# A graph network on one core: a matrix cleared with 28 stores instead of 14, and filled from three chunks later

## The reference

```python
h = relu(layernorm(x)); f = h @ W_n                        # 8 heads of 32
e = leaky(left[src] + right[dst] + edge terms) / 3         # a score per edge and head
a = exp(e - max over dst) / sum over dst                   # softmax over the edges of a node
x = x + segment_sum(f[src] * a, dst)                       # attention layer
h = relu(layernorm(x))
for l in range(3):                                         # three message layers
    msg = relu(h @ pW[l] + pb[l])[src]
    mean = segment_sum(msg, dst) / max(degree, 1)
    out = mean @ lW[l] + lb[l] + h @ rW[l]
    h = out / norm(out)                                    # silu behind the first two
return x + layernorm(h) * ln_w + ln_b
```

## Time and profile before

| | us |
|---|---|
| median of three runs | 3459.19 |
| lowest and highest of them | 3453.91, 3459.5 |
| profiled execution, its own time | 3451.81 |
| its span in the trace | 3450.0 |
| attention stage of GpSimd, first gather to last scattered write | 101.7 to 1457.4 |
| busy in the span: TensorE, GpSimd, VectorE, ScalarE | 2900.8, 2527.9, 1542.9, 1377.4 |

### The profile page before, as it was taken

One profiled execution on the slowest core, in us unless ns is written; L12 is line 12 of the kernel. 1 busy time (PEld: TensorE's weight loads), 2 busy tenths in 40 slices (PEclk: granted clock), 3 DMA queues, 4 the chain that ended last, 5 costly groups with the idle time before them and its releaser, 6 DMA issues. The chain is left out here.

```text
span 3450.0 us, 44783 instructions
## 1 busy us (share of the span) xinstructions
PE 2900.8 (84%) x12845; PEld 1770.6 (51%) x12845; DVE 1542.9 (45%) x5381; ACT 1377.4 (40%) x3235; POOL 2527.9 (73%) x2655
## 2 busy tenths in 40 slices
PE   7688877777777777199999997999999888999984
PEld 5577656656555655044455553444555433445542
DVE  6399655555555556113333232232333423445445
ACT  5366655555554555033333332333333322222220
POOL 2677777777777777777777776777777767777775
PEclk9688988888888888599999999999999999999995
DMA  7898766666666664166666654666666456667663
GB/s 218 228 281 256 204 171 178 171 169 174 179 168 177 173 169 125 42 195 182 184 194 194 201 173 143 183 180 183 199 196 201 147 171 190 197 199 221 208 187 108
DMA packets 491898, 631.26 MB, mean 183 GB/s; under 512 B 163477, under 2 KB 402096, under 8 KB 491648
## 3 DMA queue, kind: packets, MB, share of 16 engines
q0 software_dynamic: 122192, 324.68, 34.0%
q1 hardware_dynamic: 340848, 277.92, 27.2%
q10 hardware_dynamic: 28608, 25.71, 2.3%
HBM read 558.00 MB, written 70.05 MB: 182 GB/s over the span
## 5 line engine op out<-in xcount | busy, mean ns | idle before, releaser
L1218 POOL DMA_INDIRECT ring<-message_table,src_index x1545 | 1469.8, 951 | 502.5 <-issue 481.1
L1269 PE MATMUL ps<-ring,attention_work 128*128 128x384 f32 (+1 forms) x2940 | 1149.5, 538 | 85.3 <-DMA attention_work<-message_table 75.1
L604 POOL DMA_INDIRECT ring<-attention_table,src_index x784 | 763.1, 973 | 245.6 <-issue 245.2
L1269 PEld LDWEIGHTS ps<-ring,attention_work 128*128 128x128 f32 x2940 | 551.5, 192 | 555.7 <-issue 286.4
L1814 PE MATMUL ps<-ring,one_hot 128*128 128x265 f32 x1568 | 533.1, 458 | 19.7 <-issue 18.6
L1580 ACT ACTIVATE ring<-one_hot 128x384 f32<-128x384 uint8 (+1 forms) x735 | 362.0, 553 | 195.7 <-PE ps L1269 132.9
L1814 PEld LDWEIGHTS ps<-ring,one_hot 128*128 128x128 f32 x1568 | 314.7, 221 | 85.6 <-issue 49.6
L1339 PE MATMUL ps<-ring,attention_work 128*32 128x256 f32 x3090 | 256.6, 402 | 103.7 <-DMA ring<-message_table,src_index 103.4
L613 POOL DMA_INDIRECT dense_adjacency<-times,cell x277 | 269.5, 973 | 84.4 <-issue 84.4
L1434 DVE SCALAR_TENSOR_TENSOR block_o<-ps,inv_deg,root 128x256 f32<-128x256 f32 x147 | 71.1, 484 | 546.8 <-PE ps L1307 546.8
L1783 PE MATMUL ps<-ring,ident 128*128 128x224 f32 x224 | 95.7, 519 | 254.7 <-DMA ring<-attention_table,src_index 254.6
(11 more groups left out here) (185 smaller groups left out, 3500.7 us busy)
## 6 DMA issues: line engine op xcount, KB each, us to landing
attention_work<-message_table SPq DMA_DIRECT2D x360, 256.0 KB
attention_work<-in_dst_edges SPq DMA_DIRECT2D x112, 448.0 KB
ring<-message_table,src_index POOLq DMA_INDIRECT x1545
one_hot<-dense_adjacency SPq DMA_DIRECT2D x63, 336.0 KB, 4.0
one_hot<-dense_adjacency SPq DMA_DIRECT2D x42, 448.0 KB, 4.5
attention_sums<-sums_out SPq DMA_DIRECT2D x112, 132.5 KB
dense_adjacency<-root SPq DMA_DIRECT2D x14, 952.0 KB
ring<-attention_table,src_index POOLq DMA_INDIRECT x784
```

The costliest lines, as they stand in the source:

```text
L604: pool.indirect_dma_start(m.ring[:, k, t, 0:cols], None, table, bass.IndirectOffsetOnAxis(ap=m.src[:, at:at + 1], axis=0)).then_inc(s[f"ro ...
L1218: pool.indirect_dma_start(m.quad_ring[:, k, j, :], None, m.tables[w.l], bass.IndirectOffsetOnAxis(ap=m.src[:, t:t + 1], axis=0)).then_inc( ...
L1269: last = nc.tensor.matmul(m.ps[:, 2 + half, 0:cols], m.m_rows[:, u % HELD_ROWS, half * P:(half + 1) * P], m.a_rows[:, k, 0:cols], start=(j ...
```

## The change

The matrix is cleared with 28 stores of two pieces each, one in each of steps 1 to 28 of SyncE's loop, where it was 14 stores of four pieces in steps 1 to 14. The bytes and the order of the pieces stay the same. The first scattered writes, and with them GpSimd's wait for the stores, stand behind the gathers of chunk 30, not 27. The 193 writes that are spread go over 82 chunks, not 85.

```diff
@@ -89,7 +89,7 @@
 COUNT_FROM = 1
 COUNT_ROOT = 32
 ZEROS = 476
-ZERO_STORES = 14
+ZERO_STORES = 28
 LINE = CHUNKS * TILES
 REAL = E - (P - 1) * LINE
 REACH = P + 2 * RUN
@@ -101,7 +101,7 @@
 BUNCHES = 2
 HELD_ROWS = 8
 HELD_PAIRS = HELD_ROWS // 2
-ZERO_FROM, BUILD_FROM, LATE_CELLS = 1, 27, 84
+ZERO_FROM, BUILD_FROM, LATE_CELLS = 1, 30, 84
 LISTS_FROM = 14
 ROW = WIDE + HEADS * KINDS
 SUMC = WIDE + 1
```

## The result

The changed kernel takes 3476.0 us (median of five runs, 3475.0 to 3476.9), against 3455.8 us for the kernel before in five runs (3453.1 to 3459.5). The ratio is 1.0061, with a 95% interval of 1.0051 to 1.0072: 20 us slower. The profiled execution took 3474.98 us with a span of 3473.2.

What follows compares the result with a forecast made beforehand. GpSimd's list was taken to bound the attention stage; the last store, issued at 400.6 plus 4.5 us, against GpSimd ready at 388.3 gives a 16.8 us stall. Added to 3451.8 or 3459.2 us: 3468.6 or 3476.0, called 3475, range 3466 to 3484.

Steps and rivals of the forecast that it cites:

- What bounds the kernel: Attention stage: GpSimd's list runs without a gap; each microsecond it stands still moves the sweeps and the end by one.
- When GpSimd is ready: Before its first scattered write, behind 21 more gathers of 1.25 us (chunks 28 to 30): 388.3 us, before 362.07.
- When the last store is issued: SyncE's step 28, behind the loads for chunk 33: 400.6 us, bounds 2 us less and 4 us more.
- the chain that I had hold it: Ahead of SyncE's last store: L1719 waits for ScalarE, that for TensorE, that for chunk 29's gather; moves up 5.1 us.
- The remark that the added stores can slow loads: SyncE's steps 15 to 28: added stores can slow loads and gathers and so the chain; bound 4 us more.
- How long it takes: The last store of zeros, from issue until GpSimd goes on: 4.5 us, ends 3.4 and 7.7 us.
- The sum: GpSimd's first scattered write: goes on at 405.1 instead of 388.3 us, one stall of 16.8 us, neither hidden nor won back.
- the larger stall: Rival at GpSimd's wait: the last store comes late, stall 24 us, up to 27, time 3483 to 3486 us; chance 0.11.
- TensorE's one wait: TensorE at the late gather of chunk 31: waits about 10 us once, which costs nothing more.
- The hidden stall: Rival at GpSimd's wait: last store there by 395.2 us, no measurable difference, 3459 us; chance 0.09.
- The stores in series: Rival on the 14 added stores: each pays 2.5 us one behind the other, 35 us, 3494 us; chance 0.02.
- the stores slow the gathers: Rival on the gathers beside stores of zeros: halving the stores gains 6 to 12 us, 3453 to 3447 us; chance 0.04.

Runs made afterwards that it cites:

- e2: The changed kernel (28 stores) with the first scattered write in chunk 33, not 30; first run; ratio 0.9990 to the kernel before.
- e2b: The changed kernel (28 stores) with the first scattered write in chunk 33, not 30; second run; ratio 0.9991 to the kernel before.
- e6: The changed kernel with 14 full-size stores in every second step to step 28, first write in chunk 30; ratio 1.0048 to the kernel before, 20 us.
- e1: The kernel before (14 stores) with the first scattered write in chunk 30, not 27; ratio 0.9992 to the kernel before.
- v4: The kernel before with 164 writes behind the last chunk, not 84; ratio 0.9974 to the kernel before.

## Why the prediction was right, step by step

**What bounds the kernel:** right. GpSimd's list has no gap but the new one, and the sweeps moved with its end: 23.6 us later at their start, 23.2 at the end of the kernel.

**When GpSimd is ready:** forecast 388.3 us for its first write, measured 390.1 (the last gather ends at 389.8, and 0.3 us lie between two instructions). The 21 gathers were counted rightly; 0.7 us comes from a later start of the stage and 1.1 from the gathers before, the six long ones above all: 20.7 us together, before 19.5.

**When the last store is issued:** forecast 400.6, measured 408.0 us. This is the term that was mis-sized, by 7.4 us, and it is beyond my bound of 4 us more. The forecast moved the chain of the kernel before up by 5.1 us and let nothing else in it change. The queue in front of the last store was right (L1688, L1695, L1719, L1703), but the step that failed is the chain that I had hold it, through TensorE, ScalarE's L2039 and L2056 and SyncE's L1719, in "a queue that mostly waits for ScalarE". From 345 us on SyncE does not wait for ScalarE any more. It waits for the landing of the sums ahead of L1710, which the prediction did not count: 17.1 us in four places between 293 and 410 us, before 8.4. These 8.7 us more are enough for the 7.4, and I had expected the queue's delay to be 0.4 us. The remark that the added stores can slow loads named the cause in a general way, but its bound was too small. The trace of the changed kernel shows these waits; that removing them brings the 7.4 us back was not shown, since the runs made for it came to chips whose traces hardly have them.

**How long it takes:** forecast 4.5, measured 4.3 us. The rule of the Trainium skill (DMA: Bandwidth & Descriptors, "Anatomy of one DMA — SWDGE (gpsimd) path") gave an estimate of 3.1. The trace has 3.5 us to the landing and 0.8 more to GpSimd's next write. The estimate is near where the DMA engines are not full; where they were busy at 0.98, stores of this size took 5.7 to 8.0 us.

**The sum:** 16.8 + 7.4 - 0.2 - 1.8 = 22.2 us, and the gap beyond the usual 0.30 is 22.3. That is outside the 12 to 21 us that I gave the forecast and the 15 to 19 that I named as its sign, and nearer to the larger stall's 24. The time forecast, 3475 us, is 1 us under the one measured, and that nearness is luck: the stall came out 5.5 us larger, but the kernel before had a median of 3455.8 over five runs, not 3459.2, and the medians lie 20 us apart, not 22. The place of the loss and its reason were foreseen, its size was not. TensorE's one wait was forecast at about 10 us and is 21.4; it cost nothing, as said.

**The rivals.** The hidden stall did not occur. The larger stall is half true: the last store came late, though not by the 7.7 us to land. The stores in series are refuted by e2, e2b and e6. That the stores slow the gathers is refuted by the trace: with half as many bytes stored between 145 and 293 us, a gather takes 1069 ns in the mean, before 1057. All six long gathers are still there, from 3.05 to 3.88 us, each beside an L632. This agrees with the Trainium skill (SBUF — State Buffer, the part on the shared port pair). But two of the six gathers, at 174.96 and 204.36 us, start 0.2 us ahead of their L632 and are held all the same (3.88 and 3.85 us); no run here shows at which point of a gather it needs the ports.

## What to carry to other kernels

A wait costs nothing only as long as what it waits for is early. If a transfer that another engine waits for is cut up and spread over more steps, find the step in which the last piece is issued, put it beside the moment at which the waiter arrives, and move the waiter too: three chunks were too few here, and six were enough on the second kind of chip; on the first kind that was not run. A background transfer must also not be taken to be free for the foreground transfers beside it: with the DMA engines busy at 0.98 a store of sums took 6.3 to 6.7 us to land, at 0.65 it took 2.6 to 3.0, and a queue that waits for such landings hands the delay on.

## What the runs showed of the hardware that was not expected

The same kernel takes 3456 us in one group of runs and 4169 to 4177 us in the others. GpSimd and VectorE are not busier (in the kernel before and in e1: GpSimd 2527.9 and 2521.2 us, VectorE 1542.9 and 1550.8). TensorE is: 2900.8 and 3236.3 us for the same 12845 products, at a mean granted clock of 0.913 and 0.834 (a mean of stretches at 2.4 and at 1.2 GHz). Whether the lower clock comes before TensorE's pauses or from them no run shows, but the longest waits below begin behind the end of the product that is waited for, so a slower product doesn't make them. The packets of GpSimd's queue take as long in both (34.0% of 16 engines over 3450 us and 27.7% over 4165 us, both 0.15 us for each of 122192). What is new are waits that the trace ends by "remote", that is by no instruction that it can name. GpSimd's in e1, over the span:

```profile
POOL ring L604 <- remote: 158.7, 69, 3.2
POOL ring L1218 <- remote: 315.9, 138, 7.6
```

All those of over 1 us ahead of L604, 68 of them, stand ahead of the first gather of a chunk, where GpSimd waits for TensorE's sums. And nearly all the idle time of this name in e1, on whichever engine, is on semaphores that TensorE raises. The case with the clearest rows is the second chunk of e1, TensorE first, then ScalarE, which waits for this work:

```profile
123.14 3.03 PE L1775 MATMUL ps<-attention_work 128*128 128x32 f32 x14
```

```profile
165.11 1.04 ACT L2017 ACTIVATE attention_work<-attention_work,window_p 128x896 f32<-128x896 int32 x1 [46.33 <-remote]
```

TensorE's products end at 126.2 us, and ScalarE goes on at 165.1. For the sums of all chunks (L1822), the semaphore rises 0.01 us after the product's end in the median of the trace of before, 5.9 us in e1 and 3.9 us in the changed kernel on this kind of chip. While ScalarE stood still, GpSimd issued gathers without a pause, and ended just before:

```profile
160.54 0.95 POOL L604 DMA_INDIRECT ring<-attention_table,src_index  x1 [0.30 <-issue]
195.08 0.94 POOL L604 DMA_INDIRECT ring<-attention_table,src_index  x1 [33.59 <-PE ps L1814]
```

The waits of 67 and 73 us in v4 beside its 164 writes look the same. There TensorE's products themselves stand apart in the trace, in steps of 2.1 or 2.8 us:

```profile
1511.54 0.60 PE L1814 MATMUL ps<-ring,one_hot 128*128 128x265 f32 x1 [2.20 <-issue]
1514.34 0.60 PE L1814 MATMUL ps<-ring,one_hot 128*128 128x265 f32 x1 [2.20 <-issue]
1516.44 0.60 PE L1814 MATMUL ps<-ring,one_hot 128*128 128x265 f32 x1 [1.50 <-issue]
```

Whether the products ran so or only their records were late can't be told from this trace. So it seems that in these runs TensorE, or its releases alone, are held up while GpSimd issues without a pause, and that this is a large part of the 20%. That GpSimd is the cause is a reading of the traces, for which no run was made. Against it stands that in the profile of before GpSimd issues its first gathers just as closely, 1.25 us apart, and nothing is held up. Why one group of runs has none of it stays open.
